# Decoder layer on one core: mask and bias rows in stacks of 128 rows, prepared flat by GpSimd through a scratch tensor, and context masking one slot later

## The reference

```python
x = x + gated_delta_attention(layernorm(x))                  # 16 heads, a recurrent state, one output projection
x = x + cross_attention(layernorm(x), ctx_2048, mask, mask)  # 16 heads of 8 channels
x = x + ffn(layernorm(x))                                    # a shared expert and 8 routed ones, the top 2 used
```

```python
q = einsum('oc,bct->bot', Wq, target) + bq[None, :, None]    # target, source: 128 channels x 256 places per batch
k = einsum('oc,bcs->bos', Wk, source) + bk[None, :, None]
v = einsum('oc,bcs->bos', Wv, source) + bv[None, :, None]
dot = einsum('bhdt,bhds->bhts', q, k) / sqrt(8)
mask = target_mask[:, :, :, None] * source_mask[:, :, None, :]
dot = mask * dot - (1.0 - mask) * 1e6
out = einsum('bhts,bhds->bhdt', softmax(dot) * mask, v)
```

## Time and profile before

| | us |
|---|---|
| three runs: lowest, median, highest | 912.39, 912.83, 914.94 |
| span of the profiled execution | 912.7 |
| TensorE matmuls busy | 826.9 (91%) |
| TensorE weight loads busy | 532.5 (58%) |
| VectorE busy | 720.9 (79%) |
| ScalarE busy | 615.2 (67%) |
| GpSimd busy | 537.3 (59%) |

### The profile page before, as it was taken

The page is one execution under the profiler, slowest core; times in us unless marked ns, Lnnn a source line. Parts: engine busy times, 40 slices in busy tenths (PEclk is TensorE's granted clock), DMA queues, the critical chain, the costliest instruction groups (busy, mean ns, idle before and its releaser), DMA issues. The chain is left out here.

```text
span 912.7 us, 22004 instructions
## 1 busy us (share of the span) xinstructions
PE 826.9 (91%) x7421; PEld 532.5 (58%) x7458; DVE 720.9 (79%) x1227; ACT 615.2 (67%) x1020; POOL 537.3 (59%) x689
## 2 busy tenths in 40 slices
PE   3777999999999999999999999997989999988997
PEld 1344777667766777676766777675645333323353
DVE  8588887888888888888888888885545888872746
ACT  3566888788877888788778888785332277765522
POOL 6447669687696886967869669667302134321300
PEclk9798999999999999999999999998978999976999
DMA  5302010110100101101011010000000160000000
GB/s 144 112 1 82 2 36 6 32 36 0 34 25 9 34 0 34 34 0 34 0 34 34 0 34 0 12 3 1 2 1 0 28 108 22 20 21 15 11 23 24
DMA packets 34416, 23.98 MB, mean 26 GB/s; under 512 B 5062, under 2 KB 33414, under 8 KB 34235
## 3 DMA queue, kind: packets, MB, share of 16 engines
q1 hardware_dynamic: 31643, 19.00, 7.3%
q0 software_dynamic: 2720, 4.29, 2.3%
HBM read 22.68 MB, written 1.05 MB: 26 GB/s over the span
## 5 line engine op out<-in xcount | busy, mean ns | idle before, releaser
L1025 DVE SCALAR_TENSOR_TENSOR y<-psum,cwh,y 128x508 f32<-128x508 f32 (+2 forms) x384 | 281.7, 740 | 24.0 <-ACT y L701 18.0
L491 POOL TENSOR_TENSOR ct<-lm,levels 128x256 f16<-128x256 f32 x224 | 151.6, 698 | 12.0 <-DVE lm L1048 12.0
L477 POOL TENSOR_TENSOR sql<-sq,sqh 128x1024 f16<-128x1024 f32 x32 | 68.3, 2135 | 120.2 <-ACT sq L748 120.2
L701 ACT ACTIVATE y<-psum,cwh 128x512 f32<-128x512 f32 x128 | 99.3, 776 | 49.9 <-PE psum L1312 49.9
L1341 PE MATMUL psum<-wo,vt 128*128 128x256 f32 x512 | 126.0, 389 | 1.2 <-DVE y L1025 1.2
L1341 PEld LDWEIGHTS psum<-wo,vt 128*128 128x128 f32 x512 | 92.3, 190 | 11.9 <-DVE y L1025 2.0
L1164 DVE TENSOR_REDUCE mx<-psum 128x4 f32<-128x1024 f32 x64 | 77.7, 1221 | 13.4 <-PE psum L1630 13.1
L1005 DVE TENSOR_TENSOR ux<-ux,psum 128x512 f16<-128x512 f16 x64 | 43.9, 686 | 55.2 <-PE psum L1425 54.0
L822 ACT ACTIVATE et<-psum 128x1024 f32<-128x1024 f32 x64 | 65.4, 1022 | 32.0 <-PE psum L1651 31.0
L1312 PE MATMUL psum<-xth,whi 128*128 128x512 f16 x256 | 80.3, 397 | 7.2 <-POOL wlo L458 2.9
L1312 PE MATMUL psum<-xtl,whi 128*128 128x512 f16 x256 | 79.5, 393 | 0.0
(11 more groups left out here) (215 smaller groups left out, 1953.2 us busy)
## 6 DMA issues: line engine op xcount, KB each, us to landing
wraw<-in_L_attn_Wv SPq DMA_DIRECT2D x32, 128.0 KB, 2.9
wo<-in_L_attn_Wo SPq DMA_DIRECT2D x16, 256.0 KB, 2.8
wraw<-in_L_attn_Wk SPq DMA_DIRECT2D x16, 128.0 KB, 2.6
wraw<-in_L_attn_Wq SPq DMA_DIRECT2D x16, 128.0 KB, 2.9
moved<-avs SPq DMA_DIRECT2D x128, 16.0 KB, 1.8
x<-in_x SPq DMA_DIRECT2D x8, 128.0 KB, 4.0
maskrow<-in_mask_row POOLq DMA_DIRECT2D x1, 1024.0 KB, 5.3
xt<-in_ctx SPq DMA_DIRECT2D x1, 1024.0 KB, 6.0
```

The source lines that it names most:

```text
L477: g.tensor_tensor(lo, f, hi, ALU.subtract).then_inc(sq_split, 1)
L491: g.tensor_tensor(dst, src, pick.unsqueeze(1).to_broadcast([P, NB, T // (2 * m), m]), ALU.mult).then_inc(masked[l], 1)
L701: s.activation(y[:, n], ubank[n % 2].rearrange("p (j t) -> p j t", j=NB), ACT.Identity, scale=cwh[:, (a.c // 2) % 2, n, TAPS - 1:TAPS], bi ...
L1025: v.scalar_tensor_tensor(out=y[:, n, :, sh:], in0=u[:, :, 0:T - sh], scalar=cwh[:, (a.c // 2) % 2, n, TAPS - 1 - sh:TAPS - sh], in1=y[:, n ...
```

## The change

The rows of mask and bias are no longer built by VectorE on 4 and 5 partitions. The host hands the mask and the two distinct bias rows over flat, spread on 128 partitions; GpSimd takes high and low parts there in five small operations at the end of slot -1; SyncE stores them to a DRAM scratch tensor, in slot 0, and loads the rows back from it in slot 1. The tiles `biasr` and `maskr` have 128 rows, of which rows 5 and up of `biasr` are zero and rows 4 and up of `maskr` are one; GpSimd fills them at the start. The K projection's bias matmul now uses all 128 rows, the Q projection's still 4. The masking of the context moves from the end of slot 29 to the end of slot 30. VectorE and TensorE wait for the loads at the first batch of `kv`.

```diff
-    a = np.zeros((P, 4), np.float32)
+    a = np.zeros((P, 2), np.float32)
...
-        bias5 = sb("bias5", [5, 2, 4, P], F16)
-        mask5 = sb("mask5", [5, B, H], F16)
+        biasr = sb("biasr", [P, 2, 4, P], F16)
+        maskr = sb("maskr", [P, B, H], F16)
+        mflat = sb("mflat", [P, B * H // P], F32)
+        bflat = sb("bflat", [P, 2, 8], F32)
+        mhl = sb("mhl", [P, 2, 2, B * H // P], F16)
+        bhl = sb("bhl", [P, 5, 8], F16)
...
+                if k.i is None and k.c == 0:
+                    sp.wait_ge(rows_blank, 2)
+                    sp.wait_ge(rows_split, 5)
+                    sp.dma_start(d["mask_scratch"].rearrange("a b (p n) -> p a b n", p=P), mhl[:]).then_inc(rows_stored, 16)
+                    sp.dma_start(d["bias_scratch"].rearrange("a (p n) -> p a n", p=P), bhl[:]).then_inc(rows_stored, 16)
                 if k.i is None and k.c == 1:
+                    sp.wait_ge(rows_stored, 32)
+                    sp.dma_start(maskr[0:4].rearrange("p b n -> p (b n)"), d["mask_scratch"].rearrange("a b n -> (a b) n")).then_inc(rows_ready, 16)
+                    sp.dma_start(biasr[0:5].rearrange("p k g n -> p (k g n)"), d["bias_scratch"]).then_inc(rows_ready, 16)
                     sp.wait_ge(gate_psum, 1)
...
+            g.memset(biasr[:].rearrange("p k g n -> p (k g n)").bitcast(F32), 0.0).then_inc(rows_blank, 1)
+            g.memset(maskr[:].rearrange("p b n -> p (b n)"), 1.0).then_inc(rows_blank, 1)
             pool.wait_ge(consts_loaded, 16 * 7)
...
-                             (wks[:], d["xk"]), (wvt[:], d["xv"]), (stackcol[:], d["stackcol"]), (biasf, d["xbias"]),
+                             (wks[:], d["xk"]), (wvt[:], d["xv"]), (stackcol[:], d["stackcol"]), (mflat[:], d["mask_flat"]), (bflat[:], d["xbias"]),
...
+                def flat_rows():
+
+                    pool.wait_ge(xattn_loaded, 16 * 9)
+                    m = mflat[:].unsqueeze(1).to_broadcast([P, 2, B * H // P])
+                    w = bflat[:, 0:1].to_broadcast([P, 2, 8])
+                    g.tensor_copy(mhl[:, :, 0], m).then_inc(rows_split, 1)
+                    g.tensor_copy(bhl[:, 0:2], w).then_inc(rows_split, 1)
+                    g.tensor_copy(bhl[:, 4], bflat[:, 1]).then_inc(rows_split, 1)
+                    pool.wait_ge(rows_split, 2)
+                    g.tensor_tensor(mhl[:, :, 1], m, mhl[:, :, 0], ALU.subtract).then_inc(rows_split, 1)
+                    g.tensor_tensor(bhl[:, 2:4], w, bhl[:, 0:2], ALU.subtract).then_inc(rows_split, 1)
...
                 cut(b0, 5)
-                if k.i is None and k.c == STEPS - 3:
+                if k.i is None and k.c == -1:
+                    flat_rows()
+                if k.i is None and k.c == STEPS - 2:
                     pool.wait_ge(ctx_loaded, 16)
-                    pool.wait_ge(xattn_loaded, 16 * 8)
...
-            pool.wait_ge(bias_ready, 1)
...
-            v.memset(mask5[:], 1.0).then_inc(mask_cast, 1)
...
-                def prepare_bias():
-                def prepare_mask():
...
+                    if bb == 0:
+                        dve.wait_ge(xattn_loaded, 16 * 9)
...
-                prepare_bias()
-                prepare_mask()
...
-                        pe.wait_ge(mask_ready, 1)
-                        pe.wait_ge(bias_ready, 1)
+                        pe.wait_ge(xattn_loaded, 16 * 9)
+                        pe.wait_ge(rows_ready, 32)
...
-                            mm = t.matmul(o, bias5[:, 1, 2 * hh + g2], mask5[:, bb], start=False, stop=True)
+                            mm = t.matmul(o, biasr[:, 1, 2 * hh + g2], maskr[:, bb], start=False, stop=True)
...
-                mm = t.matmul(o, bias5[0:4, 0, 2 * hh + g2], mask5[0:4, b], start=False, stop=True)
+                mm = t.matmul(o, biasr[0:4, 0, 2 * hh + g2], maskr[0:4, b], start=False, stop=True)
...
-    host["xbias"] = bias
+    host["xbias"] = bias[[0, 4]].reshape(2, P, 8).transpose(1, 0, 2)
+    host["mask_flat"] = a["mask_Bx1x2048_fk1"].reshape(P, B * H // P)
...
+    for n, shape in (("mask_scratch", (2, 2, B * H)), ("bias_scratch", (5, 8 * P))):
+        d[n] = nc.dram_tensor(n, shape, F16, kind="Internal").ap()
```

More of the change, by code:

```diff
@@ L63, in constants @@
     row = r % 32
-    a = np.zeros((P, 4), np.float32)
+    a = np.zeros((P, 2), np.float32)
     a[:, 0] = np.where(((row >= 8) & (row < 16)) | (row == 27), -1.0, 0.0)
     a[:, 1] = np.where((row >= 16) & (row < 24), -1.0, 0.0)
-    a[0:4, 2] = (0.0, 0.0, -1.0, -1.0)
-    a[0:4, 3] = (0.0, -1.0, 0.0, -1.0)
     c["stackcol"] = a
@@ L144, in build @@
         epsc = sb("epsc", [P, 1], F32)
-        stackcol = sb("stackcol", [P, 4], F32)
+        stackcol = sb("stackcol", [P, 2], F32)
         maskrow = sb("maskrow", [P, B, H], F32)
@@ L209, in build @@
         kh = lb("kh", [P, 2, 2 * H], F16)
-        zrow = vv[0:5].rearrange("p b s n -> p (b s n)")
-        biasf = zrow[:, 0:8 * P].rearrange("p (k g n) -> p k g n", k=2, g=4)
-        biash = zrow[:, 8 * P:12 * P].bitcast(F16).rearrange("p (k g n) -> p k g n", k=2, g=4)
         loop.close()
@@ L309, in build @@
         xdone, result = sem("xdone"), sem("result")
-        kv_names = ("ctx_loaded", "ctx_masked", "mask_cast", "mask_ready", "bias_cast", "bias_ready", "k_psum", "k_high", "k_stack", "v_psum", "v_ready")
-        ctx_loaded, ctx_masked, mask_cast, mask_ready, bias_cast, bias_ready, k_psum, k_high, k_stack, v_psum, v_ready = [sem(n) for n in kv_names]
+        kv_names = ("ctx_loaded", "ctx_masked", "rows_blank", "rows_split", "rows_stored", "rows_ready", "k_psum", "k_high", "k_stack", "v_psum", "v_ready")
+        ctx_loaded, ctx_masked, rows_blank, rows_split, rows_stored, rows_ready, k_psum, k_high, k_stack, v_psum, v_ready = [sem(n) for n in kv_names]
         x_names = ("x_masked", "q_psum", "q_high", "q_stack", "max_psum", "max_done", "max_scaled", "max_split", "row_psum", "q_full",
```

## The result

The changed kernel took 889.12 us as the median of four runs (881.33 to 890.23), the kernel before 912.89 (912.39 to 914.94): a ratio of 0.9711, with a 95% interval of 0.968 to 0.9742. The forecast was 889.0.

The account below looks back on a forecast made before the run. TensorE was taken to bound the loop. Ramp-up 7.0, masking 4.3, 128 rows 7.0 and clock 5.5 sum to 23.8 us off 912.7: 888.9, as a median 889.0, range 882 to 897 (0.58), outer ends 880 and 903.

Parts of the forecast that it names:

- The bound: Steady loop: TensorE, busy 18.2 of 19 us a slot, bounds it, so gains of the first slots reach the end.
- Ramp-up: Slots -1 to 1: VectorE's two blocks go, GpSimd limits next; 5.7 us plus 1.3 of clock, together 7.0.
- Queues: Added stores, loads, memsets and DMA issues delay nothing that counts: taken as 0, head 2's weights bounded at 0 to 4 us.
- Rival B: Slot 0: stores hold up head 2's weights by 4 us and GpSimd hands all of it on: 893.0 us; chance 0.10.
- Masking: Slots 30 and 31: moving it wins 5.6 us, less 1.3 to 1.7 for a new wait; 4.3 taken.
- 128 rows: K projection: each projection and bias pair saves 0.22 us by hidden weight loads, times 32 pairs, 7.0 us.
- Rival A: K projection: 128 rows alter neither spacing nor clock, only waits are won, 11.8 us: 901.0 us; chance 0.14.
- Clock in the K projection: Slot 32: TensorE's low clock is back up after some 5 us, not 17; 5.5 us gained of 6.7 at stake.
- C: Slot 32: loads overlap but the clock stays low as before, 5.5 us lost: 894.5 us; chance 0.10.
- D: Attention: the clock falls on entering and does not come back, costing 40 us more: 929 us; chance 0.05.
- Low: Lower outer end of the forecast: clock term at its bound, loads at 0.26, ramp at 8.5, giving 880 us.

Follow-up runs that it names:

- oldprep: Changed kernel but with bias and mask rows still prepared by VectorE in slots -1 and 0, no flat rows or scratch tensor; 896.68 us.
- again: The changed kernel run once more, unaltered, to see its scatter; 888.97 us.
- mask29: Changed kernel with the context masking back at the end of slot 29; 888.57 us.
- k64rows: Changed kernel with the K projection's bias matmul on 64 rows instead of 128; 899.66 us.
- k5rows: Changed kernel with the K projection's bias matmul on 5 rows again; 906.6 us over seven runs.
- combined: Changed kernel with flat_rows moved ahead of sq_low_ in slot -1 and the masking split in halves over slots 30 and 31; 882.99 us.

## Why the prediction was right

Its number was right because two errors cancelled, which was luck; the mechanisms were mostly right.

1. **The bound.** TensorE is busy 18.4 of 19 us in a steady slot (95 to 114), and the loop carries the ramp's gain to the end: oldprep's loss of 8.5 us at the `sql` behind slot 0 (98.19 against 89.68; 7.2 against the 90.95 of the run again) is a loss of 7.7 at the end.
2. **Ramp-up, forecast 7.0, found 7.6.** No VectorE blocks, GpSimd next, norms at 74.57 (forecast 75.6), 6.75 us earlier. `flat_rows` was mis-sized: 1.3 taken, 0.84 measured, because its five operations start 0.14 to 0.20 us apart, where the four of `parts_`, the nearest row, start 0.27 to 0.46 apart in the trace of before. The clock gave more than the 1.3 taken: it is at 1.00 from 44 to 618 us, and where the trace of before was low for 10.2 us (59 to 63, 80 to 87), nothing is; the second profile of the changed kernel has 3.4 us there.
3. **Queues.** Taken at nothing, and right: the stores' issues took 0.37 and 0.51 us, head 2's weights were issued from 58.87, and the operation on them at 65.53 has no idle: GpSimd worked from 55.63 through slot 0 in one piece. Rival B fell here. The memsets at the start lie in GpSimd's wait for the constants, whose idle shrinks from 6.25 to 4.40 us, and nothing waits for the loads back into the tiles.
4. **Masking, forecast 4.3, found nothing. This is the step that failed.** Its first half was in the main right: TensorE's 4.13 us of idle in slot 30 went, but 3.9 us of the forecast 5.6 appeared (618.82 against 622.70 in mask29), with half of the low clock still there. The new wait ahead of `b_t1(1)` was forecast at 1.5 and measured 1.67, released by a `cut` as foretold. What failed was the sentence "I take 4.3": it let the wait in slot 31 cost only its own length. That wait also brought a dip of the clock (640 to 644), and mask29, the control with the longer wait earlier, had lost only 1.1 us more by the start of the attention, and none at the end. I had counted the clock behind the old wait as gain and none behind the new one. The sum also took off only 1.3, the smaller end of its own 1.3 to 1.7.
5. **128 rows, forecast 7.0, found 7.2 of work** (7.1 by k64rows against again). Projection 0.43 and bias 0.11 as forecast; the 0.08 that I added for a fp32 load behind a fp16 matmul did not appear. The prediction also cited the Trainium skill here, page "TensorE: Matmul & The Clock Gate", section "What overlaps and what doesn't", by which a weight load of all rows stays exposed. This case's traces show the reverse for this pattern: the full-row load at 646.80 is hidden, and the loads exposed are those of 5 and 64 rows among matmuls of 128. Rival A fell with it; k5rows is what A would have been, and at 906.6 us it lies above the 901.0 given for A, which counted 4.8 us for the masking that did not come.
6. **Clock in the K projection, forecast 5.5, found 10.7.** I looked for it in slot 32 alone and at one profile's 17 us. Over the runs, 5 rows cost 30.7 us of low clock against 128, in slot 31 as well and in part at places not seen. That the clock comes back with 128 rows was right, and the size wrong by a factor of two, which paid for step 4. Why fewer rows mean more low clock was not measured by itself: in k5rows the exposed loads and the few-row matmuls come together.
7. **Rivals C and D.** Neither came. The stretches at the low clock late in the attention add up to 27.3 us in the changed kernel (787 to 797, 801 to 818) and to as much before (810 to 824, 828 to 841).

In all, the forecast priced 17 us of waits and spacing (in the masking's 4.3 with some low clock) and 7 of clock; the runs gave 14.2 and 11.4. The outer ends hold a slip: the bounds named for "Low" (clock 6.7, loads 0.26 a pair, ramp 8.5) take 4 us off the forecast and give 885, not 880.

## What to carry to other kernels

When a short fp16 matmul sits between long ones of 128 rows, give it 128 rows too (zeros on one side are enough): what it costs otherwise is not its own length but two weight loads that do not overlap, and the clock on top. Look at both neighbours first: in the Q projection, where scores of 32 rows stand ahead, the same edit freed only part of the loads and was worth about nothing. Moving a block past a wait moves the wait: ask where the block is needed next, and whether it can be cut in two, before booking the old wait as gain. Compare kernels by several runs with their mean clock beside them, and split a difference into clock and work before giving it a cause.

## What the runs showed of the hardware beyond what I expected

- **Half the rows are as bad as five.** Loads of 5 and of 64 rows between matmuls of 128 rows are exposed alike (0.84 us a pair); with 128 rows the pair takes 0.54.
- **The low clock makes most of the scatter between runs.** 0.35 us of time per us at 1.2 GHz, well under the half that a TensorE busy all the time would lose, so part of that time lies where TensorE waits anyway. In the K projection it was more, 0.42: the stretch took 41.3 us in again and 38.4 in the first profile, with 6.8 us more at the low clock. The shortest runs of the changed kernel (881.33) and of combined (876.42, 876.80) have 28, 21 and 25 us of low clock, where the other runs of these two kernels have 39 to 53; they are 7 to 8 us shorter than these. Where in those executions the clock held was not seen, since none of them was profiled.
- **Many small stores cost their queue little.** 1,152 pieces of 16 and 32 bytes, counted from the shapes, held it for under 1 us of issue, 0.37 + 0.51, landed 1.9 and 3.3 us after it, and delayed nothing that waits behind them.
